# Attention kernel, one core: each maximum's pair of matmuls is split around the step's score matmuls, and the scores' row halves swap places

## The reference, cut to what matters

```python
def _attend(q, k, v):
    sc = q.shape[-1] ** (-0.5)
    a = jax.nn.softmax(jnp.einsum('bhnd,bhmd->bhnm', q, k) * sc, axis=-1)
    o = jnp.einsum('bhnm,bhmd->bhnd', a, v)
```

## Time and profile before

| | before |
|---|---|
| runs, us | 2233.14, 2235.68, 2239.04 (median 2235.68) |
| profiled execution, span us | 2231.9 (its time as a run is not recorded; it is 3.8 under the median) |
| TensorE busy | 2023.5 us, 91% |
| VectorE busy | 1546.2 us, 69% |
| ScalarE busy | 1287.3 us, 58% |
| GpSimd busy | 565.3 us, 25% |
| mean granted TensorE clock | 0.940 |

### The profile page before, as it was taken

The page is one execution under the profiler, slowest core; times in us unless marked ns, Lnnn a source line. Parts: engine busy times, 40 slices in busy tenths (PEclk is TensorE's granted clock), DMA queues, the critical chain, the costliest instruction groups (busy, mean ns, idle before and its releaser), DMA issues. The chain is left out here.

```text
span 2231.9 us, 33892 instructions
## 1 busy us (share of the span) xinstructions
PE 2023.5 (91%) x12890; PEld 793.8 (36%) x12890; DVE 1546.2 (69%) x2841; ACT 1287.3 (58%) x2406; POOL 565.3 (25%) x537
## 2 busy tenths in 40 slices
PE   5899898997979899998999989999998999999976
PEld 3333223332323353533533432332253335334415
DVE  5767697796957659376366557986747995896704
ACT  1145576574746677754775652678335884685670
POOL 1035776661132301033022322310204001102100
PEclk8689999998989999999999996999699999999998
DMA  7733413322052202025014522200211020000000
GB/s 155 150 71 101 124 65 101 98 66 46 19 135 63 75 4 56 17 63 125 9 53 106 94 55 78 59 21 11 45 31 30 18 40 13 13 12 8 13 16 11
DMA packets 97338, 126.67 MB, mean 57 GB/s; under 512 B 25325, under 2 KB 82014, under 8 KB 92046
## 3 DMA queue, kind: packets, MB, share of 16 engines
q1 hardware_dynamic: 94862, 123.89, 23.4%
q10 hardware_dynamic: 2304, 0.53, 0.1%
HBM read 89.95 MB, written 24.74 MB: 51 GB/s over the span
## 5 line engine op out<-in xcount | busy, mean ns | idle before, releaser
L1683 ACT ACTIVATE PT<-ps 128x512 f32<-128x512 f32 (+1 forms) x2112 | 1101.3, 602 | 722.6 <-PE ps L1468 715.9
L1766 DVE TENSOR_REDUCE mx<-ps 128x1 f32<-128x512 f32 x2048 | 1284.3, 683 | 278.6 <-PE ps L1489 275.4
L1489 PE MATMUL ps<-KS,QS 49*128 49x512 bf16 x2048 | 525.0, 403 | 127.5 <-DVE mx L1766 76.1
L1468 PE MATMUL ps<-QS,KS 51*128 51x512 bf16 (+3 forms) x4224 | 616.0, 390 | 12.0 <-DMA QS<-mr 11.6
L1515 PE MATMUL ps<-PT,Vt 128*32 128x512 f32 (+1 forms) x4224 | 585.3, 627 | 0.0
L1489 PEld LDWEIGHTS ps<-KS,QS 49*128 49x128 bf16 x2048 | 145.9, 95 | 718.4 <-DVE mx L1766 470.3
L1468 PEld LDWEIGHTS ps<-QS,KS 51*128 51x128 bf16 (+3 forms) x4224 | 209.9, 97 | 269.3 <-ACT PT L1683 87.3
L2000 POOL CAST nm<-nm 128x16 bf16<-128x16 f32 x64 | 12.7, 198 | 529.0 <-DVE nm L1779 528.8
L1515 PEld LDWEIGHTS ps<-PT,Vt 128*32 128x32 f32 (+1 forms) x4224 | 84.2, 109 | 148.3 <-issue 145.7
L1610 PE MATMUL ps<-XT,big 128*128 128x256 f32 x512 | 125.6, 396 | 2.3 <-ACT big L1739 1.4
L1622 PE MATMUL ps<-big 128*128 128x256 f32 x512 | 114.8, 382 | 1.6 <-DVE big L1901 1.6
(11 more groups left out here) (110 smaller groups left out, 1103.0 us busy)
## 6 DMA issues: line engine op xcount, KB each, us to landing
scr<-S SPq DMA_DIRECT2D x27, 768.0 KB, 3.8
big<-in_mask_1x1xSxS_ik SPq DMA_DIRECT2D x16, 1024.0 KB, 5.0
QS<-scr SPq DMA_DIRECT2D x32, 384.0 KB, 9.1
KS<-scr SPq DMA_DIRECT2D x24, 384.0 KB, 8.7
QS<-scr SPq DMA_DIRECT2D x32, 256.0 KB, 6.0
ON<-Oe SPq DMA_DIRECT2D x256, 32.0 KB, 1.9
OD<-scr_r SPq DMA_DIRECT2D x32, 256.0 KB
KS<-scr SPq DMA_DIRECT2D x24, 256.0 KB, 4.7
```

Source lines behind the costliest of these rows:

```text
L1468: z = eng.matmul(ps[0:w, it.bank[j], :], KS[lo:hi, part, pr, col:col + w], QS[lo:hi, part, u.qs, pr, :], start=part == 0, stop=part == 1 a ...
L1489: return eng.matmul(mbank(it)[:, 0:w], QS[lo:lo + MR, 0, u.qs, pr, 128 * it.tq:128 * it.tq + 128], KS[lo:lo + MR, 0, pr, it.lo:it.hi], sta ...
L1683: eng.activation(PT[0:w, it.pt * 4 + 2 * it.pp + j, :], ps[0:w, it.bank[j], :], ACT.Exp, scale=0.25).then_inc(S["exp_done"], 1)
L1766: eng.tensor_reduce(out=mx[:, u.b, c, it.i:it.i + 1], in_=mbank(it)[:, 0:it.hi - it.lo], axis=AX.X, op=ALU.max).then_inc(S["max_done"], 1)
```

## The change

In `quantum` and `narrow` the two halves of a task become two functions. In a step, all tasks but the last are put in whole; then the first half of the last task, then the step's scores, then its second half, on even and odd steps alike. The scores are issued with row half 1 ahead of row half 0, and the banks, the exponentials and P times V follow that swap. `fin_a` is a task of one function. What ran on other lines is the same, eight lines further down.

```diff
             def quantum(pp, tq, i, lo, hi):
-                for j in range(2):
+                def half(j):
                     it = item("max")
...
+                return [lambda: half(0), lambda: half(1)]
...
-                    odd = step % 2 == 1
-                    if odd:
-                        f()
                     if not left and k + 1 < total and (k == 0 or step >= opens[k]):
...
+                    now_ = []
                     if left:
                         want = m if step - lo >= span else -(-(step - lo) * m // span)
                         while m - len(left) < min(want, m):
-                            left.pop(0)()
-                    if not odd:
-                        f()
+                            now_.append(left.pop(0))
+                    for task in now_[:-1]:
+                        for g in task:
+                            g()
+                    for g in now_[-1][:1] if now_ else ():
+                        g()
+                    f()
+                    for g in now_[-1][1:] if now_ else ():
+                        g()
...
                     for part in range(2):
-                        for j in range(2):
+                        for j in (1, 0):
                             s_half(it, j, part)
...
-                    for j in range(2):
-                        q.wait_ge(S["s_ready"], it.s[j])
-                        eng.activation(PT[0:w, it.pt * 4 + 2 * it.pp + j, :], ps[0:w, it.bank[j], :], ACT.Exp,
+                    for k in range(2):
+                        q.wait_ge(S["s_ready"], it.s[k])
+                        eng.activation(PT[0:w, it.pt * 4 + 2 * it.pp + 1 - k, :], ps[0:w, it.bank[k], :], ACT.Exp,
                                        scale=0.25).then_inc(S["exp_done"], 1)
```

More of the change, by code:

```diff
@@ L387, in narrow @@
                     u.last = it
+                return [lambda: half(0), lambda: half(1)]
             if early is not None:
                 for i, (lo, hi) in enumerate(parts):
-                    tasks.extend(early[i:i + 1])
-                    tasks.extend(lambda a=(pp, tq, i, lo, hi): quantum(*a) for pp in range(2) for tq in range(4))
+                    tasks.extend([e] for e in early[i:i + 1])
+                    tasks.extend(quantum(pp, tq, i, lo, hi) for pp in range(2) for tq in range(4))
             for pp in range(2) if early is None else ():
@@ L395, in max_tasks @@
                     if hi - lo < 128:
-                        tasks.append(lambda a=(pp, i, lo, hi): narrow(*a))
+                        tasks.append(narrow(pp, i, lo, hi))
                 for tq in range(4):
@@ L399, in max_tasks @@
                         if hi - lo >= 128:
-                            tasks.append(lambda a=(pp, tq, i, lo, hi): quantum(*a))
+                            tasks.append(quantum(pp, tq, i, lo, hi))
             def fin_a():
@@ L428, in fin_b @@
                 fins.append([FIN - 1, lambda: plan.append(it)])
-            return tasks + [fin_a]
+            return tasks + [[fin_a]]
         def exp_steps(u, held):
@@ L459, in pv @@
                 it.u, it.i = u, i
-                it.x = [xs[i, 0] - 1, xs[i, 0], xs[i, 1] - 1, xs[i, 1]]
+                it.x = [xs[i, 0], xs[i, 0] - 1, xs[i, 1], xs[i, 1] - 1]
                 it.o_free = n["o_free"]
@@ L795, in attention @@
             if first:
-                for j, f in enumerate(start(0, early)):
-                    f()
+                for j, task in enumerate(start(0, early)):
+                    for f in task:
+                        f()
                     fin_step()
@@ L839, in attention @@
                     while left:
-                        left.pop(0)()
+                        for g in left.pop(0):
+                            g()
                     fin_step(True)
@@ L1466, in s_half @@
                 if part == 0:
-                    q.wait_ge(S["exp_done"], it.a_need[j])
-                z = eng.matmul(ps[0:w, it.bank[j], :], KS[lo:hi, part, pr, col:col + w], QS[lo:hi, part, u.qs, pr, :],
+                    q.wait_ge(S["exp_done"], it.a_need[1 - j])
+                z = eng.matmul(ps[0:w, it.bank[1 - j], :], KS[lo:hi, part, pr, col:col + w], QS[lo:hi, part, u.qs, pr, :],
                                start=part == 0, stop=part == 1 and not u.ph.masked, tile_position=(lo, 0))
                 if part == 1 and u.ph.masked:
-                    z = eng.matmul(ps[0:w, it.bank[j], :], negI[:], maskT[:, vt, :], start=False, stop=True)
+                    z = eng.matmul(ps[0:w, it.bank[1 - j], :], negI[:], maskT[:, vt, :], start=False, stop=True)
                 if part == 1:
```

1 line of the change is left out of this document (removed).

## The result

| | before | after |
|---|---|---|
| median of the runs, us | 2234.41 (2229.82 to 2239.04, 4 runs) | 2208.31 (2205.17 to 2213.70, 4 runs) |
| profiled execution: span, us | 2231.9 | 2203.3 (2205.17 as a run) |
| mean granted TensorE clock | 0.940 | 0.945 |

The ratio of the medians is 0.9891 with a 95% interval of 0.9869 to 0.9914: 26 us less, between 19 and 29. The forecast was 2217 us with a range of 2204 to 2235. The direction and the place were right. The amount was not: 18.9 us were summed, 26.1 came between the medians and 28.6 between the two profiled spans.

The account below looks back on a forecast made before the run. TensorE and VectorE were taken as nearly balanced, coupled by three banks; terms 11.4 + 1.3 + 1.4 + 0.4 + 3.3 - 1.3 - 0.6 + 3.0 = 18.9 us off 2231.9 left 2213, runs about 2217 us, range 2204 to 2235.

Parts of the forecast that it names:

- The opening tiles: Tiles where a unit opens (SSSS SSSS MMMM): four scores fill the last M's wait, 3.36 to 2.92 us, 26 x 0.44 = 11.4 us.
- Usual tiles: 256 of 528 tiles, 2.49 us each: no gain; 0.18 us of slack remain before the third M's bank.
- tiles with T: 43 tiles with a transpose that takes a bank: no gain, the fourth M still 1.76 us after the first.
- rival of the stalled third M: Third M stalls in usual tiles with scores and fourth M behind it: slower, 2255 us if 0.15 per tile; chance 0.05.
- the one in which the waits only move: VectorE comes later into tiles behind an opening one, handing back the 0.44: no difference, 2229 to 2236 us; chance 0.13.
- 65-key tiles: Last M waits for the first 65-key reduction; four scores now cover it: 0.44 in 6 tiles, 0.18 in 4, 3.3 us gained.
- losses: Three tiles whose third M waits for ScalarE's hidden-layer activation, with four scores now behind it: +0.44 x 3 = 1.3 us.
- term for second M: Second M waiting for something other than reductions: 1.3 us behind hidden-layer blocks, 1.4 behind transposes, 0.4 once behind a longer wait.
- two tiles behind a DMA: M of a new chunk waits for a DMA; scores that ran before it now come after: 0.6 us lost.
- Crowded stretches: Twice 26 tasks in 8 steps: VectorE's gaps partly cut, partly widened, between 6 us lost and 8 won; 3 won taken.
- The clock: TensorE waits shift low-clock time: 30 us less adds 11 us (2206 us); 55 more eats the gain, chance of that 0.04.
- The row halves: Between scores and M: unswapped order would lose half a pair, 0.1 us, at each tile boundary; swapped order nothing.

Follow-up runs that it names:

- the joined `fin_a`: `fin_a` hung on the last task instead of counting as its own, on the kernel before with no split: 2199.41 us, ratio 0.9861.

## Why the prediction was right, and where not

- **The opening tiles (11.4 us).** Right in mechanism and nearly in size: 2.92 us as forecast, 10.2 us in all the tiles at full clock that end in four M. The run with the split in steps of two or more tasks alone holds the whole gain, the one without them holds none.
- **Usual tiles and tiles with T (0).** Right: of the 256 usual tiles, 222 of 249 at full clock take 2.48 or 2.49 us before and 227 of 252 after, and most of the 43 with T stay at 3.08. The slack of 0.18 us ahead of the third M held, so the rival of the stalled third M fell, and so did the one in which the waits only move: the tiles behind an opening tile, which in layer 0 are those with T, kept their 3.08.
- **65-key tiles (3.3), losses (1.3).** Right in size: 3.3, and 1.3. The term for second M (3.1) was too high: three tiles behind a hidden-layer block gave 0.24 and five behind transposes 0.21, some 1.8. The output-projection tiles were not in the sum and cost 2.2. In one of them the first scores now idle 0.32 for the DMA of the negated maxima, which they had not waited for before. The 0.6 for the two tiles behind a DMA can't be told from the clock in those tiles.
- **Sum without the crowded stretches: 15.9.** Tiles at full clock in both traces: 15.4. That they meet so closely is partly luck: the terms above with the output projections come to 11.8, and 3.6 came in tiles to which the sum gave little or nothing, such as five with transposes between their scores (0.21 each) and two that begin with T (0.36 each).
- **Crowded stretches (3, bounds -6 to 8).** About 5, by the means of nine profiles and by the run that split them alone, but some 3 of these go with the clock. At one clock the term of 3 can't be called wrong.
- **The head: missing.** I gave it no term. It holds steps of two tasks, much of it at half clock, and lost 4 to 5 us.
- **The clock.** "Fewer waits may take some away" was the step that I priced at nothing in the forecast, and it is the one that makes up the difference. The rival said that 30 us less of low clock would bring 11 us and 2206 us; 27 us less came, worth about 10, and the measured time is 2208. So what came is the forecast and this rival together, not one of them. The crowded stretches and the head hold a part of these 10 us.
- **The forecast's own range.** 2209 to 2224 doesn't follow from the bounds that it names. From 2217, 5 us down and 9 up for the crowded stretches and 4 for the clock give 2208 to 2230.
- **The row halves.** Here the prediction's step failed: "without the swap of the row halves M on the upper half would be followed by a score on the upper half", priced at 0.1 us at each of a tile's boundaries. The split without the swap takes the same 2.49 us in a usual tile, and so does a list with three of a half in a row. The Trainium skill, in "TensorE: Matmul & The Clock Gate", section Part 3, lets a weight load overlap running matmuls only where the row group differs. The runs agree that one half alone is slow (3.26 us against 2.49), and disagree with reading it as a rule on neighbours in the list. What the order does change is when a result comes: the first exponential 0.21 us earlier in the changed kernel, worth 2.6 us, and the M behind a score of its own half 0.12 later in eleven opening tiles of the swap alone.

## What to carry to other kernels

Look for the tile in which the same buffers are claimed four times in a row with nothing between: the independent work beside it belongs into that wait, and all other tiles can stay as they are. Ask first why that tile is so dense. Here a bookkeeping item counted as a task made it so, and moving that item was worth more (33 us) than reordering around it (26 us). Where two row halves of the array run side by side, keep their shares equal over a tile. A strict alternation isn't needed for that; let the order be set by which result the next engine needs first. And when a gain exceeds the waits that were counted, compare the mean granted clock of many executions before looking for another mechanism.

## What the runs showed of the hardware

- Matmuls of 51 and 49 rows on different row halves need not alternate: 0 1 0 1, 1 0 1 0 and 0 0 1 1 inside a twelve-matmul tile with six on each half all give 2.49 us; with ten on one half it is 3.26 us. The order moves the first exponential from 1.92 to 1.71 us behind P times V.
- A matmul on an idle half is recorded as starting before older ones of the busy half (340.85 against 341.06).
- In 143 executions of 13 kernels, 1 us more at the lower clock goes with 0.36 us more of time within a kernel whose TensorE is at half clock for 10 to 12% of the span.
- Tiles at full clock gained 15.4 us (15.9 summed) and, for the joined `fin_a`, 25.3 (25 expected), while the medians moved by 26 and 33, 11 and 7 us more. At 0.36, the lower share of low clock is worth about 10 and 6 us of the two.
